# One mixer and feed-forward layer on one core: all four mixers first, and every feed-forward batch by seven products

## The reference

```python
# mixer, x: (4, 512, 512)
i, f, g = x @ Wi.T, x @ Wf.T, x @ Wg.T
gate = sigmoid(f)
v = silu(i) * (1.0 - gate)
o[t] = gate[t] * o[t - 1] + v[t]              # scan along the rows of a batch
o = o * rsqrt(mean(o * o) + EPS) * gnorm_w * g * sigmoid(g)
y = o @ Wo
# feed-forward, D = 512, H = 2048
hidden = silu(x @ W1.T) * (x @ W3.T)
hidden = fwht(hidden)                          # Walsh-Hadamard transform along H
out = hidden @ W2.T
# layer
x = x + layernorm(mixer(layernorm(x)))
x = x + layernorm(feed_forward(layernorm(x)))
```

## Time and profile before

| | |
|---|---|
| median of three runs | 685.01 us |
| the profiled execution's span | 683.7 us |
| PE busy | 665.8 us (97%) |
| VectorE busy | 479.8 us (70%) |
| ScalarE busy | 292.7 us (43%) |
| GpSimd busy | 261.6 us (38%) |
| granted TensorE clock, mean | 0.999 |

### The profile page before, as it was taken

How to read it: one execution, slowest core, us unless ns; L and a number is a source line. 1 busy time by engine, 2 the same in 40 slices (tenths; PEclk the granted TensorE clock), 3 DMA queues, 4 the chain that set the end, 5 groups by cost and what they waited for, 6 DMA issues and landing times.

```text
span 683.7 us, 10835 instructions
## 1 busy us (share of the span) xinstructions
PE 665.8 (97%) x4068; PEld 403.8 (59%) x4068; DVE 479.8 (70%) x836; ACT 292.7 (43%) x482; POOL 261.6 (38%) x228
## 2 busy tenths in 40 slices
PE   3999999999999999999999999999999999999996
PEld 2344454444444454567777785657567777777762
DVE  6998889988999878857577463456576555752554
ACT  4898974675245217623232312344234222321231
POOL 1189689558356200534422300233346211111231
PEclk9999999999999999999999999999999999999999
DMA  8961311413789985638496362202526846144122
GB/s 334 393 246 70 135 47 47 139 61 109 236 325 257 233 252 195 227 147 283 143 253 237 108 169 108 108 32 93 199 95 186 184 170 220 36 157 173 57 72 92
DMA packets 58819, 113.29 MB, mean 166 GB/s; under 512 B 33424, under 2 KB 37776, under 8 KB 54160
## 3 DMA queue, kind: packets, MB, share of 16 engines
q1 hardware_dynamic: 58768, 112.61, 49.7%
HBM read 81.92 MB, written 23.07 MB: 154 GB/s over the span
## 4 chain that ended last, share of the span: by engine, by line
PE 93%; DMA 3%; POOL 1%; SPq 1%; DVE 1%; issue 0%; ACT 0%; POOLq 0%; DVEq 0%
PE ps L611 30%; PE ps L613 30%; PE ps L612 30%; PE ps L759 2%; DMA w2t<-W2t 2%; DMA ring<-L_attn_Wf 1%; SPq L518 1%; PE ps L661 1%; POOL w2t L1420 1%; PE ps L720 0%; POOL rstd L1377 0%; POOL x1r L1420 0%; SPq L483 0%; ACT ot L861 0%; PE ps L683 0%
## 5 line engine op out<-in xcount | busy, mean ns | idle before, releaser
L611 PE MATMUL ps<-xb,ring 128*128 128x256 f16 (+1 forms) x704 | 226.0, 321 | 0.4 <-DVE ring L1105 0.4
L613 PE MATMUL ps<-xb,ring 128*128 128x256 f16 (+1 forms) x704 | 225.9, 321 | 0.0
L612 PE MATMUL ps<-xb,ring 128*128 128x256 f16 (+1 forms) x704 | 225.9, 321 | 0.0
L612 PEld LDWEIGHTS ps<-xb,ring 128*128 128x128 f16 x704 | 68.9, 98 | 48.1 <-issue 2.9
L611 PEld LDWEIGHTS ps<-xb,ring 128*128 128x128 f16 x704 | 69.1, 98 | 47.8 <-issue 2.6
L1377 POOL TENSOR_TENSOR rstd<-var,neg_half 128x1 f32<-128x1 f32 x64 | 45.3, 712 | 128.5 <-DVE var L1355 42.6
L613 PEld LDWEIGHTS ps<-xb,ring 128*128 128x128 f16 x704 | 68.9, 98 | 42.1
L1434 POOL TENSOR_TENSOR ring<-sga,ring 128x512 f16<-128x512 f32 x36 | 44.1, 1231 | 106.7 <-ACT ring L1019 106.7
L611 PE MATMUL ps<-ring 128*128 128x256 f16 x288 | 78.5, 273 | 0.0
L613 PE MATMUL ps<-ring 128*128 128x256 f16 x288 | 78.5, 273 | 0.0
L612 PE MATMUL ps<-ring 128*128 128x256 f16 x288 | 78.5, 273 | 0.0
(11 more groups left out here) (174 smaller groups left out, 1193.6 us busy)
## 6 DMA issues: line engine op xcount, KB each, us to landing
ring<-w_comb SPq DMA_DIRECT2D x24, 1792.0 KB, 7.6
ring<-W13t SPq DMA_DIRECT2D x16, 512.0 KB, 7.3
ring<-W13t SPq DMA_DIRECT2D x8, 1024.0 KB, 6.1
w_comb<-ring SPq DMA_DIRECT2D x8, 1024.0 KB, 8.1
rows<-L_attn_hidden_states SPq DMA_DIRECT2D x16, 256.0 KB, 4.6
w2t<-W2t SPq DMA_DIRECT2D x8, 512.0 KB, 10.2
res<-L_attn_hidden_states SPq DMA_DIRECT2D x16, 256.0 KB, 4.5
w_comb<-ring SPq DMA_DIRECT2D x8, 512.0 KB, 2.7
```

What stands on the lines that cost most here:

```text
L611: pe.matmul(dst, a_hi, b_hi, start=start, stop=False)
L612: pe.matmul(dst, a_hi, b_lo, start=False, stop=False)
L613: return pe.matmul(dst, a_lo, b_hi, start=False, stop=stop)
```

## The change

- The four mixers come first; feed-forward batch f then works on mixer batch `MIXER_OF[f]` = 1, 2, 3, 0.
- Feed-forward batch 0 is computed by seven products like the others. The plain `GA` and `UP` steps and the four `ZT` transposes on PE are gone; the weights are prepared straight in the slots that the products read.
- The sums are formed in PSUM. ScalarE seeds the bank of `GQ` with the first product twice (`seed_p1`), and later the bank of `GP` with half of it (`seed_u2`); PE accumulates onto them. VectorE adds the fifth product to a quarter of the result in `sum_c22` and `sum_c12`, 256 columns each. `GP` now holds two products, `GQ` two, `GR` two and `GU` one.
- silu(i) and silu(g) stay in PSUM, and the scan reads its input there.
- W2's butterflies: 5 units on VectorE, 3 on GpSimd.
- All five order tables are new.

```diff
-LATE = 4
+MIXER_OF = (1, 2, 3, 0)
+RING_HID = 11
...
-GA.0.15:6 D.0.0 UP.0.15:7 D.0.1 D.0.2 D.0.3 D.0.4 D.0.5 D.0.6 D.0.7 D.0.8 D.0.9 D.0.10 D.0.11 D.0.12 D.0.13
...
+D.3.45 GP.3.14:7 GU.3.13 D.3.46 D.3.47 GQ.3.14:4 GP.3.15:6 GR.3.14 GQ.3.15:5 D.3.48 GU.3.14 GR.3.15 D.3.52 GU.3.15
+D.3.56 D.3.60 D.3.49 D.3.53 D.3.57 D.3.61 D.3.50 D.3.54 D.3.58 D.3.62 D.3.51 D.3.55 D.3.59 D.3.63
...
+            def products_p2_p6(f, g):
+                n = HC * f + g
+                pe.wait_ge(seed_rdy, n + 1)
+                dst = bank("GQ", f, g)
+                product(dst[:, 0:256], f, g, 1, 1)
+                product(dst[:, 256:512], f, g, 4, 4).then_inc(gq_mm, 1)
+
+            def products_p7_p3(f, g):
+                n = HC * f + g
+                pe.wait_ge(u2_rdy, n + 1)
+                product(bank("GQ", f, g)[:, 256:512], f, g, 5, 5).then_inc(gr_mm, 1)
+                pe.wait_ge(p5_rdy, n + 1)
+                product(bank("GP", f, g)[:, 0:256], f, g, 6, 2).then_inc(gr_mm, 1)
+
+            def product_p4(f, g):
...
+                pe.wait_ge(c22_rdy, n + 1)
...
+                product(bank("GQ", f, g)[:, 256:512], f, g, 2, 6).then_inc(up_mm if w else ga_mm, 2)
...
-                if n > 0:
-                    act.wait_ge(o_rdy, n)
-                act.activation(si[:], bank("I", b, c)[:], ACT.Silu, scale=unscale[:, 1:2]
+                act.activation(bank("I", b, c)[:], bank("I", b, c)[:], ACT.Silu, scale=unscale[:, 1:2]
...
+            def seed_p1(b, g):
+
+                n = HC * b + g
                 act.wait_ge(gp_mm, n + 1)
+                wait_for_bank(act, "GQ", b, g)
+                src = bank("GP", b, g)
+                both = src[:, 0:256].rearrange("p (o t) -> p o t", o=1).broadcast_to((P, 2, 256))
+                act.activation(bank("GQ", b, g)[:].rearrange("p (o t) -> p o t", o=2), both, ACT.Copy).then_inc(seed_rdy, 1)
                 if n > 1:
+                    act.wait_ge(c12_rdy, n - 1)
+                act.activation(p5[:, g % 2], src[:, 256:512], ACT.Copy).then_inc(p5_rdy, 1)
+
+            def seed_u2(b, g):
+                n = HC * b + g
+                act.wait_ge(gq_mm, n + 1)
+                act.wait_ge(p5_rdy, n + 1)
+                act.activation(bank("GP", b, g)[:, 0:256], bank("GQ", b, g)[:, 256:512], ACT.Copy).then_inc(u2_rdy, 1)
...
-                dve.scalar_tensor_tensor(si[:], gate[:, c % 2], 1.0, si[:], ALU.subtract, ALU.mult
+                update = bank("I", b, c)
+                dve.scalar_tensor_tensor(update[:], gate[:, c % 2], 1.0, update[:], ALU.subtract, ALU.mult
...
+            def sum_c22(b, g):
...
+                dve.tensor_tensor(summed(g)[:, 256:512], bank("GQ", b, g)[:, 256:512], p5[:, g % 2], ALU.add).then_inc(c22_rdy, 1)
+
+            def sum_c12(b, g):
...
+                dve.tensor_tensor(summed(g)[:, 0:256], bank("GP", b, g)[:, 0:256], p5[:, g % 2], ALU.add).then_inc(c12_rdy, 1)
```

More of the change, by code:

```diff
@@ L783, in product, with products_p1_p5 @@
                     b_hi, b_lo = comb_z(b, q, 0)[:, k, :], comb_z(b, q, 1)[:, k, :]
-                    last = three_passes(dst, a_hi, a_lo, b_hi, b_lo, start and k == 0, stop and k == 1)
+                    last = three_passes(dst, a_hi, a_lo, b_hi, b_lo, start and k == 0, stop and k == 1, onto)
                 return last
-            def two_products(kind, b, g, one, two, done, by=1):
+            def products_p1_p5(f, g):
                 j, w = divmod(g, 2)
-                n = HC // 2 * (b - 1) + j
-                wait_bank(kind, b, g)
-                dst = bank(kind, b, g)
-                if one:
-                    product(dst[:, 0:256], b, j, w, *one, True, False)
-                product(dst[:, 256:512], b, j, w, *two, not one, True).then_inc(done, by)
@@ L907, in g @@
                 act.wait_ge(g_mm, n + 1)
[L908 to L910 removed]
+                act.activation(bank("G", b, c)[:], bank("G", b, c)[:], ACT.Silu, scale=unscale[:, 2:3]
                                ).then_inc(sgg_rdy, 1)
@@ new lines, in yn, with zt @@
+                act.activation(y_rows(t), bank("Y", b, t)[:], ACT.Identity, bias=ab[:, 0, t:t + 1],
+                               scale=ysc[:, t:t + 1]).then_inc(y_norm, 1)
+            def zt(f, q):
+                if q < 3:
+                    act.wait_ge(z_norm, TC * f + (4 if q == 2 else 2))
+                else:
+                    act.wait_ge(z_cmb, TC * f + q - 2)
+                if f > 1:
+                    act.wait_ge(ld_zt, 16 * 7 * f)
+                elif f == 1:
+                    act.wait_ge(ms_mm, B)
+                    act.wait_ge(o_lo, KC * B)
+                else:
+                    act.wait_ge(squared, max(squares_to["WN", j, 0] for j in range(HC // 2)))
+                act.activation(parts_of_z(f, q)[:, 0], rows_of_z(q).rearrange("p i (k d) -> p k i d", k=2), ACT.Copy
+                               ).then_inc(z_hi, 1)
@@ L960, in wt @@
             def wt(c, w):
+                j = c // 2
                 if c == 0 and w == 0:
                     act.wait_ge(w_srdy, 2)
-                if w == 0 and c >= 2:
-                    act.wait_ge(wt_lo, 2 * (c - 1))
-                act.activation(ffn_w(c)[:, w, 0], ffn_raw(c)[:, w], ACT.Copy, scale=w_s[:, w:w + 1]
-                               ).then_inc(wt_hi, 1)
+                    for i in range(1, 4):
+                        act.wait_ge(aw_lo[i], KC)
+                if c % 2 == 0 and w == 0:
+                    if j >= 2:
+                        act.wait_ge(ld_s[j % 2], 16 * (j // 2))
+                    if j == 2:
+                        act.wait_ge(ld_zt, 16 * 7)
+                    if j >= SLOTS:
+                        act.wait_ge(st_s[j % SLOTS], 16 * (j // SLOTS))
+                        act.wait_ge(up_mm, 2 * (j - SLOTS) + 2)
```

852 lines of the change are left out of this document (392 added, 460 removed).

## The result

The changed kernel takes 691.81 us in the median (689.71 to 691.95), against 685.0 for the kernel before: a ratio of 1.0089, with the interval 1.0073 to 1.0105. It is slower by 0.9%, where 681.8 us and faster was forecast. The profiled execution is the short one: 689.7 us, span 687.9.

A forecast was written before the change was run, and what follows sets the result against it. The prediction took TensorE's own speed as the bound: -11.2 (its work) - 2 (head) + 3.0 (tail) + 4 (VectorE late) + 3 (handshakes) = -3.2 us, a span of 680.5 and a time of 681.8 us; range 672 to 692.

The forecast's parts named there:

- TensorE's work: Batch 0's plain matmuls become seven narrow products (-9.4 us) and four ZT steps go (-1.8): -11.2 us if TensorE stays full.
- The head: Start of the kernel: F.0.0 behind two weight norms, not three, starting near 17.3 us: -2 us, bounds -4 and +1.
- The tail: End of the kernel: no down steps cover the chain from last product to last hidden chunks: +3.0 us, up to 0.4 more.
- VectorE: Its total busy time falls from 480 to 410 us, but its work moves forward, ahead of sums TensorE needs.
- PSUM prices: Scan steps on VectorE with one operand in PSUM take their least durations: -0.97 x 16 = -15 us of VectorE.
- rival 4: Gates in PSUM don't shorten the scan; VectorE keeps 15 us and is late by 19: about 697 us, chance 0.05.
- The lateness of +4: TensorE's GU.0.10 waits for VectorE's sum of group 10 in batch 0: +4 us, bounds 0 and +18.
- handshakes: Three answers from ScalarE or VectorE in each of 64 product groups: 0.05 us a group, +3 us, bounds 0 and 10.
- rival 2: VectorE bounds the front half, slower than before, around group 10's sum: at 8.6% idle 18 us, 696 us; chance 0.22.
- rival 3: The answers TensorE waits for in product groups cost 10 us or more, with VectorE as forecast: 689 us, chance 0.10.
- the tightest 20 or so places: Product groups where TensorE has least work between question and answer (0.63 to 0.68 us); claimed just covered when the answerer is free.
- The forecast's own sign of being wrong: The forecast is wrong if TensorE's gaps after 42 us sum to under 4 or over 18 us.

## Why the forecast was wrong, point by point

- **TensorE's work**, -11.2: measured -11.1. Right.
- **The head**, -2: measured -1.1 (first start -0.8, gaps -0.3). F.0.0 starts at 18.8 us, not 17.3, and F.0.2 waits 1.55, not 1.8. Right in kind, 0.9 short.
- **The tail**, +3.0: measured 3.4, in the range given. What was missing is the clock behind it: 0, 1.4 or 2.8 us, depending on the execution.
- **VectorE**: total right to 0.2 us, PSUM prices right (rival 4 is out). The lateness of +4 was put at group 10 of batch 0; no wait stands there. What VectorE's and ScalarE's fullness costs is paid in the mixers, at 54, 55 and 80 us. With the handshakes these 42 to 280 us cost 7.2, where 4 + 3 were forecast: the sum is right by luck, since the places are others. Halving the butterflies gave back only 1.9 of it, so rival 2 is out.
- **Handshakes**, +3: the waits on the seeds are 1.2 us in all, and 24 us more of copies cost 1.4. Smaller than forecast; rival 3 is out.
- **The failed step** is in the handshakes' part: "the tightest 20 or so places are just covered when the answering engine is free". I counted what TensorE has to do between its question and the answer, and for VectorE its work in the front half. I did not look at what each answer stands behind on its own engine once the load is light. From 340 to 360 us, in batch 1, VectorE is busy for 11.4 of 20 us and yet 4 us late for one sum, since steps that wait for a store and a reload stand ahead of it. That is 4.4 us, and 1.4 for the clock; the sum of the forecast had no term for either.
- **The clock** was taken as 1.00 throughout, because before it was 1.00 at every stretch in which TensorE worked. With two more gaps, of 3.4 and some 4 us, it isn't: 1.4 us lost in the short executions, 6.2 in the longest profiled one (1.6 in the head, 1.8 behind 356, 2.8 in the tail). And of the first 20 us the row did not show the level, as said above.
- Together: 5.8 for the place at 356 us, 0.9 for the head, 0.4 for the tail, 0.2 for the rest after 372 us and about 0.5 by which the time stands further above the span than before take 681.8 to 689.6, the short executions' time. The clock makes most of the median's other 2 us, as far as the profiles show: the mean granted clock was 0.995 in the execution of 689.7 us and 0.990 or 0.991 in the three of 691.7 to 691.95, of which there is no trace.
- The forecast's own sign of being wrong, gaps behind 42 us of under 4 or over 18 us in sum, did not speak: they sum to 17.8. It was too wide to show a loss of 5.8 us at a place without a term.

## What to carry to other kernels

When an engine must answer in the middle of another's work, list for each answer what stands ahead of it in its own engine's order, and where each of those gets its data; here one step that waited for a DMA cost 4.4 us, more than all the waits on the seeds together (1.2), and it did so where the engine looks idle. Price a gap of TensorE at more than its length: here one of 3.40 us cost 3.4 to 6.2 us, by chance, and closing two gaps of 4.4 and 3.4 us was worth 8.5 us in the median. A buffer that is stored and reloaded has both transfers in its chain, here 3.5 and at most 3.9 us for 256 KB each.

## What was not expected of the hardware

- Whether the clock falls behind a gap is not told by the gap's length here. It fell behind all ten gaps of 3.3 to 8.6 us at 356 us, behind five of twelve gaps of 3.40 us in the tail (two of five in profiles of the changed kernel), and behind gaps of 2.65 and 2.89 us at 53 us, but not behind one of 3.41 us there, nor behind the 2.99 us at 356 us.
- Idle matmuls worth 1.7 us in the first 18 us made the kernel 4.8 us faster in the median.
- A store of 256 KB landed in 6.4 us with two loads of 1.8 MB issued ahead of it, and in 2.1 us with one of them; the reload of 256 KB that the other one then preceded took 8.4 us instead of at most 3.9.
